# Eight experts in the last stage of a fused attention kernel: the second product turned round, the gate weights spread by DMA

## The chip, the cores and the metric

The kernel runs on one core of one Trainium2 chip. The engines of the core work side by side, each through its own queue of instructions in program order, and wait for one another by semaphores: TensorE (PE) multiplies, with its weight loads shown apart as PEld, VectorE (DVE) and ScalarE (ACT) do elementwise work, GpSimd (POOL) does elementwise work more slowly, SyncE (SP) issues the DMAs. The metric is the time on the device of one execution in microseconds (us), median of several runs; less is better.

## What is computed

The input is 32 sequences of 100 tokens with 128 features each. A first block (attention, cross attention, a small network), a second cross attention and a gated network run first; the stage that the change touches is the last one, a self-attention layer followed by a mixture of eight experts. Cut to what matters:

```python
def _moe(x, gW, gb, W1, b1, W2, b2):          # x: 3200 tokens x 128
    gates = softmax(xf @ gW + gb)              # 8 gates per token
    top2_scores, top2_idx = top_k(gates, 2)
    w = (one_hot(top2_idx, 8) * top2_scores[..., None]).sum(1)   # 3200 x 8, two of eight not zero
    h = relu(einsum('nd,edf->enf', xf, W1) + b1[:, None, :])     # f = 256
    y = einsum('enf,efd->end', h, W2) + b2[:, None, :]
    out = einsum('ne,end->nd', w, y)
```

The result is added to x, layer-normalised, scaled by a tanh of a gate and added to an earlier value. All eight experts are computed for every token, and the gate weight w sets what each adds.

## The kernel before

Three stages run one after another; `stage_c` is the last. It works on eight units of four sequences (400 tokens). Its first loop is self-attention, 64 pieces k of half a sequence's heads; its second loop is the experts, 64 pieces n, with u, e = divmod(n, 8): unit u, expert e. The order of instructions is written by hand, engine by engine, and nothing reorders it.

In the expert loop TensorE runs, for piece n, `expert(n)` and then `hidden(n + 2)`. `hidden` (line 1906) multiplies the tokens of unit u (YT, features on the partitions) with W1: two matmuls of 128x128 weights with 400 moving columns, into two of the PSUM banks 0 to 3. ScalarE's `rectify` (line 1682) adds the bias and clips to zero into HE, which has two places, so `rectify(n)` waits until `expert(n - 2)` is through. `expert` (line 1917) takes HE as weights, 100 tokens at a time, and W2 as the moving operand: eight matmuls of 128 moving columns, result with tokens on the partitions, in bank 4 or 5 by turns. VectorE's `add` (line 2096) multiplies that with the gate weight, which is one number per partition here, and adds it into U3, four instructions a piece. The records of the trace show each such float32 matmul twice (16 records for the eight matmuls, 4 for the two).

The bias b2 enters by way of the gate weights: `turn_weights` (line 1891) turns the 100x32 weights of a unit on TensorE, ScalarE copies them to WT (`weights_turned`, line 1673), `bias` (line 1754, reached through `project`) multiplies WT with B2 into bank 7, and VectorE's `first` (line 2089) starts U3 with that sum and the residual Y. Of the unit after, these stand behind pieces 3 and 5. After a unit's last piece VectorE takes the `moments` (lines 1993 to 1998), GpSimd the power for the standard deviation (`rstd`, line 1535), VectorE the `shift` (line 2003), ScalarE normalises (`leave`, line 1603, four instructions), GpSimd scales and adds (`leave`, lines 1566 and 1569), and SP stores (line 1522). A few steps of the attention of the last unit (`turn1`, `outer`, `turn2`, `gate`, the gate chain of units 6 and 7 on VectorE) stand between the first pieces.

Of the kernel before, what the change touches and what calls it, by code (L numbers as in the profile page):

```python
# [19 lines left out]
ALU = mybir.AluOpType  # L20
# [80 lines left out]
attx_psum b2_psum back_psum big_loaded c_chain c_cleared fe_ready fk_psum fk_ready fo_psum fpT_psum fpT_ready fq_psum  # L101
fq_ready fs_psum fu_ready fv_psum fv_ready gate_psum gate_used gexp_ready gsub_ready hb_ready kbd_ready moe_h_psum
moe_h_ready moe_y_psum moe_y_used os_ready out_ready out_scaled r_used sub_ready u_ready wT_psum wT_ready w_ready
wo_psum x_ready xb_ready xin_ready y_ready y_scaled
# [9 lines left out]
def build(nc, x, ctxn, ctxt, mask, wpack, cpack, rpack, kpack, w1, w2, b2, wgu, out):  # L114
    with ExitStack() as ctx:
# [16 lines left out]
        x1 = dram("x1_scratch", [T, BATCH, D])  # L132
        h3t = dram("h3t_scratch", [D, BATCH * T])
# [54 lines left out]
        stage_c(nc, t, x1, att, w1, w2, out)  # L188
# [1256 lines left out]
def stage_c(nc, t, x1, att, w1, w2, out):  # L1445

    with ExitStack() as ctx:
# [11 lines left out]
        loaded, stored = places("c_loaded", 2), places("c_stored", 2)  # L1459
# [20 lines left out]
        WT = sb("WT", [EXPERTS, 2, TG])  # L1480
        W1 = sb("W1", [D, FT * D])
# [24 lines left out]
        def _(sp):  # L1506
# [13 lines left out]
            for u in range(UNITS):  # L1520
# [77 lines left out]
        def _(act):  # L1598
# [70 lines left out]
            def weights_turned(u):  # L1669
                act.wait_ge(sem["wT_psum"], u + 1)  # L1670
                if u >= 2:
                    act.wait_ge(sem["b2_psum"], u - 1)
                nc.scalar.copy(WT[:, u % 2, :], bank(7, EXPERTS, TG)).then_inc(sem["wT_ready"], 1)

# [48 lines left out]
            weights_turned(0)  # L1723
            for n in range(PIECES):
# [19 lines left out]
        def _(pe):  # L1744
# [105 lines left out]
            def turn1(u):  # L1850
# [3 lines left out]
                elif u < LAST:  # L1854
                    pe.wait_ge(sem["gate_used"], u)
                else:
                    pe.wait_ge(sem["u_ready"], 1)
# [7 lines left out]
            def turn2(u):  # L1865
# [5 lines left out]
                else:  # L1871
                    pe.wait_ge(sem["u_ready"], 2)
# [7 lines left out]
            def turn_weights(u):  # L1880
                pe.wait_ge(sem["w_ready"], u + 1)
                if u == 0:
                    pe.wait_ge(sem["gate_used"], LAST)
                elif u == 1:
                    pe.wait_ge(sem["r_used"], UNITS)
                elif u == 2:
                    pe.wait_ge(sem["gate_used"], UNITS)
                else:
                    pe.wait_ge(sem["u_ready"], u)
                for j in range(GROUP):  # L1890
                    x_ = nc.tensor.transpose(bank(7, EXPERTS, T, j * T), gt[:, u, 6, j * EXPERTS:(j + 1) * EXPERTS], ident[0:T, 0:T])
                x_.then_inc(sem["wT_psum"], 1)

            def bias(u):
                pe.wait_ge(sem["wT_ready"], u + 1)
                project(7, WT[:, u % 2], t.B2[:, :], sem["b2_psum"])

# [346 lines left out]
```

## Time and profile before

| | us |
|---|---|
| median of 3 runs | 2406.93 |
| lowest and highest of them | 2406.34, 2409.48 |
| time of the profiled execution | 2401.97 |
| span of its trace | 2400.2 |
| TensorE busy in the span | 2028.5 (85%) |
| VectorE busy | 1583.8 (66%) |
| ScalarE busy | 1320.0 (55%) |
| expert loop, from its first hidden matmul (2157.5) to the end | 242.7 |

Times in the trace count from the start of the span. The profiled execution ran 5.0 us under the median of the three unprofiled ones, so a sum made in the trace is carried over to the median by adding that. The granted clock (PEclk) is TensorE's clock as a share of 2.4 GHz; 0.50 is its lower level, 1.2 GHz.

### The profile page before, as it was taken

How to read it: one execution, taken by the hardware profiler on the slowest of the kernel's cores; microseconds unless marked ns; L12 is line 12 of the kernel's file. 1: busy time of each engine (PE TensorE's matmuls, PEld its weight loads, DVE VectorE, ACT ScalarE, POOL GpSimd, SP SyncE). 2: the span in 40 equal slices, each digit the busy share in tenths (PEclk: the TensorE clock that was granted, in tenths of full speed). 3: DMA queues.
4: the chain of work that ended last, by engine and by line, in shares of the span. 5: the costliest groups of instructions: out<-in, count | busy, mean ns of one | idle time of the engine just before them, and what ended most of it. 6: DMA issues, size and time to landing. Idle time of an engine off the chain costs nothing. (4 is left out here: it accounts for less than half of the span.)

```text
span 2400.2 us, 45166 instructions
## 1 busy us (share of the span) xinstructions
PE 2028.5 (85%) x17914; PEld 1347.5 (56%) x17914; DVE 1583.8 (66%) x3854; ACT 1320.0 (55%) x2169; POOL 535.9 (22%) x476
## 2 busy tenths in 40 slices
PE   3779997466599999999999999999996888878997
PEld 2546665343355556556565555556564565656776
DVE  5844543787578878877877878878862566654443
ACT  3645554576246666666666666666673555543333
POOL 1410000553302212212222212212212233221111
PEclk9789997666589999999999999999997898879999
DMA  5026662000222313313323323313312110000000
GB/s 160 1 86 187 186 186 75 4 18 17 90 69 104 115 64 113 114 64 117 107 77 108 107 72 113 115 62 115 115 43 94 35 36 18 1 1 4 8 8 11
DMA packets 89104, 181.18 MB, mean 75 GB/s; under 512 B 5907, under 2 KB 63163, under 8 KB 88511
## 3 DMA queue, kind: packets, MB, share of 16 engines
q1 hardware_dynamic: 88894, 178.30, 22.6%
q8 instruction: 143, 2.34, 0.4%
q14 instruction: 67, 0.54, 0.1%
HBM read 95.24 MB, written 11.65 MB: 45 GB/s over the span
## 5 line engine op out<-in xcount | busy, mean ns | idle before, releaser
L1408 DVE TENSOR_REDUCE b_part_max<-psum 128x1 f32<-128x482 f32 (+3 forms) x1248 | 737.3, 650 | 187.6 <-PE psum L1285 173.6
L1198 ACT ACTIVATE b_PT<-psum 128x800 f32<-128x800 f32 x768 | 616.4, 836 | 386.0 <-PE psum L1304 380.0
L1285 PE MATMUL psum<-b_KH,b_QBD 64*128 64x482 f32 (+1 forms) x1152 | 421.4, 443 | 46.3 <-DVE b_part_max L1408 43.4
L1304 PE MATMUL psum<-b_QS,b_KS 64*128 64x200 f32 x3072 | 438.7, 288 | 0.5 <-ACT b_PT L1198 0.3
L1304 PEld LDWEIGHTS psum<-b_QS,b_KS 64*128 64x128 f32 x3072 | 339.6, 186 | 16.2 <-issue 12.1
L1320 PE MATMUL psum<-b_PT,b_V 128*32 128x200 f32 x6144 | 341.1, 339 | 0.6 <-ACT b_PT L1198 0.6
L1285 PEld LDWEIGHTS psum<-b_KH,b_QBD 64*128 64x128 f32 x1152 | 196.6, 188 | 198.0 <-DVE b_part_max L1408 118.6
L1121 POOL TENSOR_TENSOR b_KL<-b_KF,b_KH 128x1444 fp32r<-128x1444 f32 x32 | 106.8, 3337 | 691.9 <-PE psum L1304 669.7
L1320 PEld LDWEIGHTS psum<-b_PT,b_V 128*32 128x32 f32 x6144 | 159.9, 109 | 149.0 <-ACT b_PT L1198 82.3
L2096 DVE SCALAR_TENSOR_TENSOR c_U<-psum,c_gt,c_U 100x128 f32<-100x128 f32 x256 | 72.1, 344 | 129.0 <-PE psum L1917 128.8
L384 POOL TENSOR_TENSOR a_rs<-a_ve,a_half 100x4 f32<-100x4 f32 x48 | 50.0, 1041 | 420.7 <-DVE a_ve L757 420.6
L1917 PE MATMUL psum<-c_W,c_HE 128*100 128x128 f32 x1024 | 123.6, 274 | 14.1 <-ACT c_HE L1682 14.0
L1917 PEld LDWEIGHTS psum<-c_W,c_HE 128*100 128x100 f32 x1024 | 117.2, 167 | 31.8 <-ACT c_HE L1682 18.7
L1272 PE MATMUL psum<-W,b_CT 128*128 128x128 f32 (+1 forms) x768 | 117.7, 293 | 12.7 <-DVE b_part_max L1408 6.7
L804 DVE TENSOR_REDUCE a_peak<-psum 100x1 f32<-100x1446 f32 x32 | 53.2, 1664 | 105.3 <-PE psum L629 105.3
L1272 PEld LDWEIGHTS psum<-W,b_CT 128*128 128x128 f32 (+1 forms) x768 | 92.7, 188 | 41.4 <-DVE b_part_max L1408 37.4
L1682 ACT ACTIVATE c_HE<-psum,C 128x400 f32<-128x400 f32 x128 | 71.9, 587 | 78.9 <-PE psum L1906 75.9
L1646 ACT COPY c_PT<-psum 100x800 f32<-100x800 f32 x64 | 52.5, 821 | 102.0 <-PE psum L1810 102.0
L636 PE MATMUL psum<-a_P,a_CN 128*128 128x100 f32 (+1 forms) x768 | 108.0, 288 | 0.0
L1261 PE MATMUL psum<-b_CT,W 128*128 128x482 f32 (+1 forms) x192 | 101.2, 611 | 5.5 <-DVE b_QF L1382 1.5
L636 PEld LDWEIGHTS psum<-a_P,a_CN 128*128 128x128 f32 (+1 forms) x768 | 95.2, 195 | 18.7 <-issue 11.8
L1535 POOL TENSOR_TENSOR c_rs<-c_ve,c_half 100x4 f32<-100x4 f32 x24 | 24.4, 1015 | 337.0 <-DVE c_ve L1998 337.0
(274 smaller groups left out, 3204.3 us busy)
## 6 DMA issues: line engine op xcount, KB each, us to landing
b_KS<-b_KH SPq DMA_DIRECT2D x64, 722.0 KB
a_CT<-in_ctxt SPq DMA_DIRECT2D x32, 722.0 KB, 4.2
b_CT<-in_ctxt SPq DMA_DIRECT2D x32, 722.0 KB, 4.3
b_KS<-b_KL SPq DMA_DIRECT2D x32, 722.0 KB
a_CN<-in_ctxn SPq DMA_DIRECT2D x32, 704.0 KB
att_scratch<-b_AO SPq DMA_DIRECT2D x32, 200.0 KB, 1.9
c_AIN<-att_scratch SPq DMA_DIRECT2D x8, 800.0 KB
b_MB<-in_mask SPq DMA_DIRECT2D x32, 180.5 KB, 4.4
```

The source lines that it names most:

```text
L636: x_ = mm(bank(7, D, T, TG), CN[0:rows, m % 3, k, :], PTA[0:rows, m % 2, k, :], start=(k == 0), stop=(k == KT - 1))
L1121: pl.tensor_tensor(KL[:, :], KF[:, 0:S], KH[:, j % 2, :].bitcast(F32), ALU.subtract).then_inc(sem["kl_ready"], 1)
L1198: nc.scalar.activation(PT[:, kt % 2, 2 * a:2 * a + 2, :], psum[:, 2 * a:2 * a + 2, 0:TG], ACT.Exp).then_inc(sem["pt_ready"], 1)
L1261: m = mm(bank(b, D, size), w("xkT"), CT[:, j % 2, c:c + size], start=True, stop=True)
L1272: m = mm(bank(b, rows, D, (k % 4) * D), CT[:, j % 2, k * D:k * D + rows], w("xvT"), start=True, stop=True)
L1285: m = mm(bank(b, D, size), QBD[rows, j % 2, tile * D:(tile + 1) * D], KH[rows, j % 2, at_:at_ + size], start=True, stop=True)
L1304: m = mm(bank(p, D, 2 * T, (s % 2) * 2 * T), KS[rows, j % 2, s, kt * D:(kt + 1) * D], QS[rows, j % 2, s * 2 * T:(s + 1) * 2 * T], start=Tr ...
L1320: m = mm(psum[32 * r:32 * r + 32, 6, b * 2 * T:(b + 1) * 2 * T], V[:, j % 2, kt, 4 * b + r, :], PT[:, kt % 2, 2 * b + r // 2, (r % 2) * 2 ...
L1408: v.tensor_reduce(part_max[0:rows, q, c:c + 1], bank(b, rows, CHUNKS[c][1]), AX.X, ALU.max)\
L1682: nc.scalar.activation(HE[:, n % 2, f, :], bank((2 * n + f) % 4, D, TG), ACT.Relu, bias=t.C[:, c:c + 1]).then_inc(sem["moe_h_ready"], 1)
L1917: x_ = mm(bank(4 + n % 2, T, D, j * D), HE[:, n % 2, f, t.ts_(j)], W2[:, c * D:(c + 1) * D], start=(f == 0), stop=(f == 1))
L2096: last = v.scalar_tensor_tensor(out=U3[:, u % 2, j, :], in0=tok_bank(4 + n % 2)[:, j, :], scalar=gt[:, u, 6, j * EXPERTS + e:j * EXPERTS + ...
```

## The change

- `expert` takes W2 as the weights and HE as the moving operand: two matmuls of 400 columns a piece, into one bank (4 or 5) for the whole unit, features on the partitions. All eight experts add up in PSUM. The bias is one more matmul of 400 columns at the unit's end, B2 as weights and WT moving.
- With tokens along the columns, a gate weight is no longer one number per partition. So it is multiplied in ahead of the product: `weigh_hidden` on VectorE, two instructions a piece, multiplies HE in place with G, in which the weights of a unit stand on all 128 partitions.
- G is made by DMA: SP writes the 100x32 weights of a unit to DRAM in turned order, waits for that, and reads them back, once spread to 128 partitions (3200 numbers each) and once as the 8x400 WT. G uses the memory of AIN for even units and of KBD for odd ones, both free by then. All this stands in SP's queue ahead of the stores.
- At a unit's end ScalarE copies the sum to YF (`experts_kept`), TensorE turns it back into bank 7 (`turn_experts`, four transposes, behind piece 4 of the next unit), and VectorE's `gather` adds the residual and takes the moments, behind piece 5. `leave` of a unit stands two units later on ScalarE.
- `turn_weights`, `weights_turned`, `bias`, `first` and `add` are gone. The gate chain of units 6 and 7 is cut into parts behind different pieces.

```diff
+            def spread_gates(u):
+                sp.wait_ge(sem["w_ready"], u + 1)
+                sp.dma_start(gates[u].rearrange("(c k) -> k c", k=T),
+                             gt[:, u, 6, :],
+                             allow_slow_non_contiguous=True).then_inc(sem["w_stored"], 16)
+                sp.wait_ge(sem["w_stored"], 16 * (u + 1))
+                if u == 0:
+                    sp.wait_ge(sem["attx_psum"], UNITS)
+                if u == 1:
+                    sp.wait_ge(sem["fs_psum"], PIECES)
+                if u >= 2:
+                    sp.wait_ge(sem["moe_g_ready"], 2 * EXPERTS * (u - 1))
+                    sp.wait_ge(sem["yT_psum"], u - 1)
+                sp.dma_start(G[u % 2].rearrange("p e k -> p (e k)"), gates[u].partition_broadcast(D)).then_inc(g_loaded[u % 2], 16)
+                sp.dma_start(WT[:, u % 2, :], gates[u].rearrange("(e k) -> e k", e=EXPERTS)).then_inc(g_loaded[u % 2], 16)
...
+            for u in range(UNITS):
+                spread_gates(u)
+                if u >= 3:
+                    store(u - 3)
+            for u in range(UNITS - 3, UNITS):
+                store(u)
...
+            def experts_kept(u):
+                act.wait_ge(sem["yT_psum"], u + 1)
+                if u:
+                    act.wait_ge(sem["y_back_psum"], u)
+                nc.scalar.copy(YF[:, :], bank(4 + u % 2, D, TG)).then_inc(sem["yT_ready"], 1)
...
+                if e == 0 and u >= 2:
+                    leave(u - 2)
                 if e == 2 and u:
-                    leave(u - 1)
-                if e == 3 and u < LAST:
-                    weights_turned(u + 1)
+                    experts_kept(u - 1)
+            experts_kept(LAST)
+            leave(LAST - 1)
             leave(LAST)
...
+            def turn_experts(u):
+                pe.wait_ge(sem["yT_ready"], u + 1)
...
+                for j in range(GROUP):
+                    x_ = nc.tensor.transpose(bank(7, T, D, j * D), YF[:, t.ts_(j)], ident)
+                x_.then_inc(sem["y_back_psum"], 1)
...
             def expert(n):
-                e = n % EXPERTS
-                pe.wait_ge(sem["moe_h_ready"], 2 * n + 2)
-                if n >= 2:
-                    pe.wait_ge(sem["moe_y_used"], n - 1)
-                for j in range(GROUP):
-                    for f in range(2):
-                        c = 2 * e + f
-                        x_ = mm(bank(4 + n % 2, T, D, j * D), HE[:, n % 2, f, t.ts_(j)], W2[:, c * D:(c + 1) * D],
-                                start=(f == 0), stop=(f == 1))
+                u, e = divmod(n, EXPERTS)
+                b = bank(4 + u % 2, D, TG)
+                if e == 0 and u >= 2:
+                    pe.wait_ge(sem["yT_ready"], u - 1)
+                for f in range(2):
+                    pe.wait_ge(sem["moe_g_ready"], 2 * n + f + 1)
+                    c = 2 * e + f
+                    x_ = mm(b, W2[:, c * D:(c + 1) * D], HE[:, n % 2, f, :], start=(e == 0 and f == 0), stop=False,
+                            skip_group_check=True)
                 x_.then_inc(sem["moe_y_psum"], 1)
+                if e == EXPERTS - 1:
+                    pe.wait_ge(g_loaded[u % 2], 32 * (u // 2 + 1))
+                    mm(b, t.B2[:, :], WT[:, u % 2, :], start=False, stop=True, skip_group_check=True).then_inc(sem["yT_psum"], 1)
...
+            def weigh_hidden(n):
+                u, e = divmod(n, EXPERTS)
+                if e == 0:
+                    dve.wait_ge(g_loaded[u % 2], 32 * (u // 2 + 1))
+                for f in range(2):
+                    dve.wait_ge(sem["moe_h_ready"], 2 * n + f + 1)
+                    v.tensor_tensor(HE[:, n % 2, f, :], HE[:, n % 2, f, :], G[u % 2][:, e, :], ALU.mult).then_inc(sem["moe_g_ready"], 1)
```

TensorE, from behind piece 3 of a middle unit, before:

```order
L1891 MATMUL psum<-K,c_gt 8x100 x4
L1917 MATMUL psum<-c_W,c_HE 100x128 x8
L1906 MATMUL psum<-c_YT,c_W 128x400 x2
L1917 MATMUL psum<-c_W,c_HE 100x128 x8
L1906 MATMUL psum<-c_YT,c_W 128x400 x2
L1754 MATMUL psum<-B,c_WT 100x128 x4
L1917 MATMUL psum<-c_W,c_HE 100x128 x8
```

and after, from behind piece 4 (L1936 is `expert`, L1925 `hidden`, L1941 the bias, L1914 `turn_experts`):

```order
L1914 MATMUL psum<-K,c_YF 100x128 x4
L1936 MATMUL psum<-c_HE,c_W 128x400 x2
L1925 MATMUL psum<-c_YT,c_W 128x400 x2
L1936 MATMUL psum<-c_HE,c_W 128x400 x2
L1925 MATMUL psum<-c_YT,c_W 128x400 x2
L1936 MATMUL psum<-c_HE,c_W 128x400 x2
L1941 MATMUL psum<-c_WT,B 128x400
L1925 MATMUL psum<-c_YT,c_W 128x400 x2
```

Eight matmuls of 128 columns became two of 400, four small bias matmuls became one, and the turning of the weights became the turning of a finished unit.

VectorE, at the turn from one unit to the next, before:

```order
L2096 SCALAR_TENSOR_TENSOR c_U<-psum,c_gt,c_U 100x128 x8
L1993 BN_STATS c_stats<-c_U 100x6 x4
L181 MEMSET carrier 1x1
L1996 BN_AGGR c_mv<-c_stats 100x2 x4
L1998 TENSOR_SCALAR c_ve<-c_mv 100x4
L2089 TENSOR_TENSOR c_U<-psum,c_Y 100x512
L2096 SCALAR_TENSOR_TENSOR c_U<-psum,c_gt,c_U 100x128 x8
```

and after, from pieces 0 to 5 of a unit (L2110 is `weigh_hidden`, two rows a piece; L2116 and what follows it `gather` of the unit before; L2022 its `shift`):

```order
L2110 TENSOR_TENSOR c_HE<-c_HE,c_AIN 128x400 x12
L2116 TENSOR_TENSOR c_U<-psum,c_Y 100x512
L2012 BN_STATS c_stats<-c_U 100x6 x4
L182 MEMSET carrier 1x1
L2015 BN_AGGR c_mv<-c_stats 100x2 x4
L2017 TENSOR_SCALAR c_ve<-c_mv 100x4
L2110 TENSOR_TENSOR c_HE<-c_HE,c_AIN 128x400 x4
L2022 SCALAR_TENSOR_TENSOR c_nb<-c_mv,c_rs 100x4
```

The product now waits for VectorE ahead of it, where VectorE had worked behind it, and the end of a unit stands five pieces later.

SP, after its last load of the attention loop, has this from the fourth unit on (L1525 writes the turned weights, L1536 and L1537 read them back, L1541 stores a unit), where it had only the eight stores:

```order
L1525 DMA gates_scratch<-c_gt 100x32x1
L1536 DMA c_KBD<-gates_scratch 128x3200
L1537 DMA c_WT<-gates_scratch 8x400
L1541 DMA out_tokens<-c_OUT 100x512
L1525 DMA gates_scratch<-c_gt 100x32x1
L1536 DMA c_AIN<-gates_scratch 128x3200
L1537 DMA c_WT<-gates_scratch 8x400
```

Each unit has three DMAs more, and the store of unit u - 3 stands behind the reading back of unit u.

## Rows read from the trace of the kernel before

**Rows 1.** Busy time, granted clock and DMA by stretch: start:end, length, engines, PEclk.

```profile
core 0: us, PE busy (x) PEld busy (x) DVE busy (x) ACT busy (x) POOL busy (x), PEclk, DMA share, GB/s
2156.00:2160.00 4.00, 3.80 (x12) 2.64 (x13) 0.62 (x4) 0.00 (x0) 0.00 (x0) 0.50 0.00 0
2250.00:2300.00 50.00, 46.93 (x304) 36.82 (x303) 20.96 (x84) 20.34 (x40) 7.11 (x6) 1.00 0.03 9
```

**Rows 2.** Timeline, two pieces: start, length, engine, line, out<-in, [idle before <-releaser].

```profile
2250.79 1.91 PE L1917 MATMUL psum<-c_W,c_HE 128*100 128x128 f32 x16
...
2252.53 1.51 PE L1906 MATMUL psum<-c_YT,c_W 128*128 128x400 f32 x4
...
2253.41 1.26 ACT L1682 ACTIVATE c_HE<-psum,C 128x400 f32<-128x400 f32 x2 [1.83 <-PE psum L1906]
...
2253.88 1.91 PE L1917 MATMUL psum<-c_W,c_HE 128*100 128x128 f32 x16
```

**Rows 3.** Timeline of TensorE, one middle unit from its piece 4.

```profile
2238.17 0.51 PE L1891 MATMUL psum<-K,c_gt 100*8 100x100 f32 x4
2240.21 1.99 PE L1917 MATMUL psum<-c_W,c_HE 128*100 128x128 f32 x16 [1.53 <-ACT c_HE L1682]
...
2246.57 1.11 PE L1754 MATMUL psum<-B,c_WT 8*100 8x128 f32 x8
...
2268.29 1.99 PE L1917 MATMUL psum<-c_W,c_HE 128*100 128x128 f32 x16 [1.53 <-ACT c_HE L1682]
```

**Rows 4.** Timeline of TensorE, units 0 and 1.

```profile
2157.52 2.96 PE L1906 MATMUL psum<-c_YT,c_W 128*128 128x400 f32 x4
...
2163.17 1.99 PE L1917 MATMUL psum<-c_W,c_HE 128*100 128x128 f32 x16
...
2168.50 1.99 PE L1917 MATMUL psum<-c_W,c_HE 128*100 128x128 f32 x16 [1.65 <-ACT c_HE L1682]
...
2202.70 1.99 PE L1917 MATMUL psum<-c_W,c_HE 128*100 128x128 f32 x16 [1.56 <-ACT c_HE L1682]
...
2225.80 1.91 PE L1917 MATMUL psum<-c_W,c_HE 128*100 128x128 f32 x16
```

**Rows 5.** Timeline, from the last addition to the last store.

```profile
2388.88 1.12 DVE L2096 SCALAR_TENSOR_TENSOR c_U<-psum,c_gt,c_U 100x128 f32<-100x128 f32 x4 [0.62 <-PE psum L1917]
...
2391.61 1.02 POOL L1535 TENSOR_TENSOR c_rs<-c_ve,c_half 100x4 f32<-100x4 f32 x1 [14.18 <-DVE c_ve L1998]
...
2392.92 1.65 ACT L1603 ACTIVATE c_OUT<-c_U,c_nb,c_rs 100x128 f32<-100x128 f32 x4 [7.01 <-DVE c_nb L2003]
...
2397.27 0.29 SPq L1522 DMA_DIRECT2D out_tokens<-c_OUT  x1
```

**Rows 6.** VectorE groups by shape: line, op, shapes, count, busy us, mean ns, idle.

```profile
L2022 DVE TENSOR_TENSOR c_P<-psum,c_peak 100x400 f32<-100x400 f32 x128 | 67.4, 568 | 2.2
...
L2089 DVE TENSOR_TENSOR c_U<-psum,c_Y 100x512 f32<-100x512 f32 x8 | 5.5, 690 | 4.9 <-PE psum L1754 4.9
```

**Rows 7.** Timeline where VectorE and GpSimd read SBUF at once, and where not.

```profile
39.20 0.57 DVE L777 TENSOR_TENSOR a_P<-K,a_sm 100x400 f32<-100x400 f32 x1
...
1840.12 1.26 POOL L1539 TENSOR_TENSOR c_XIN<-c_XIN,c_rows 100x512 f32<-100x512 f32 x1
1840.19 1.22 DVE L2003 SCALAR_TENSOR_TENSOR c_nb<-c_mv,c_rs 100x4 f32<-100x4 f32 x1 [1.14 <-POOL c_rs L1535]
```

**Rows 8.** That VectorE line over the whole trace: duration ns min/median/max, first and last start.

```profile
L2003 DVE SCALAR_TENSOR_TENSOR c_nb<-c_mv,c_rs x24: 151/158/1220, 1840.2 to 2392.7; 100x4 f32<-100x4 f32 x24
```

**Rows 9.** DMA in 1787 to 1794, small copies alone: packets, MB, share of 16 engines.

```profile
q1 hardware_dynamic: 36, 0.01, 0.7%
```

**Rows 10.** DMA in 2397 to 2400.2, one store of 100 rows of 2 KB.

```profile
DMA packets 110, 0.20 MB, mean 64 GB/s; under 512 B 10, under 2 KB 10, under 8 KB 110
...
q1 hardware_dynamic: 110, 0.20, 21.7%
```

**Rows 11.** DMA in 2010 to 2018, one load of AIN and XIN.

```profile
q1 hardware_dynamic: 254, 1.02, 38.9%
```

More of the change, by code:

```diff
@@ L132, in build @@
         x1 = dram("x1_scratch", [T, BATCH, D])
+        gates = dram("gates_scratch", [UNITS, EXPERTS * TG])
         h3t = dram("h3t_scratch", [D, BATCH * T])
@@ L187, in build @@
         stage_b(nc, t, ctxt, mask, pen_dram, h3t, att)
-        stage_c(nc, t, x1, att, w1, w2, out)
+        stage_c(nc, t, x1, att, gates, w1, w2, out)
 def setup(nc, t, mask, wpack, cpack, rpack, kpack, b2, wgu, pen_dram):
@@ L1442, in _, with stage_c @@
             drain(END, 0, GROUPS - 1, GROUP + 1, "result", 0)
-def stage_c(nc, t, x1, att, w1, w2, out):
+def stage_c(nc, t, x1, att, gates, w1, w2, out):
     with ExitStack() as ctx:
@@ L1519, in _, with store @@
                 load(u)
-            for u in range(UNITS):
+            def spread_gates(u):
[13 more added lines that the diff above has]
+                sp.dma_start(WT[:, u % 2, :], gates[u].rearrange("(e k) -> e k", e=EXPERTS)).then_inc(g_loaded[u % 2], 16)
+            def store(u):
                 sp.wait_ge(sem["out_ready"], u + 1)
                 sp.dma_start(out[:, u * GROUP:(u + 1) * GROUP, :], OUT[:, u % 2, :, :]).then_inc(stored[u % 2], 16)
+            for u in range(UNITS):
[4 more added lines that the diff above has]
+                store(u)
             for place in range(2):
@@ L1959, in _ @@
             hidden(0)
-            turn_weights(0)
             hidden(1)
-            bias(0)
             for n in range(PIECES):
@@ L1975, in _ @@
                     gate(LAST)
-                if e == 3 and u < LAST:
-                    turn_weights(u + 1)
-                if e == 5 and u < LAST:
-                    bias(u + 1)
+                if e == 4 and u:
+                    turn_experts(u - 1)
+            turn_experts(LAST)
         @block.vector
@@ L2082, in gate_weights, with gather @@
                 link(last)
-                v.tensor_tensor(gt[:, u, 6, :], gt[:, u, 2, :], gt[:, u, 5, :], ALU.add).then_inc(sem["w_ready"], 1)
-            def first(u):
-                dve.wait_ge(sem["b2_psum"], u + 1)
+                v.tensor_tensor(gt[:, u, 6, :].rearrange("p (e j) -> p j e", j=GROUP), ge(u, 2), ge(u, 5), ALU.add).then_inc(sem["w_ready"], 1)
+            def weigh_hidden(n):
[5 more added lines that the diff above has]
+                    v.tensor_tensor(HE[:, n % 2, f, :], HE[:, n % 2, f, :], G[u % 2][:, e, :], ALU.mult).then_inc(sem["moe_g_ready"], 1)
+            def gather(u):
+                dve.wait_ge(sem["y_back_psum"], u + 1)
                 if u >= 2:
@@ L2090, in first @@
                 dve.wait_ge(sem["u_ready"], u + 1)
-            def add(n):
-                u, e = divmod(n, EXPERTS)
-                dve.wait_ge(sem["moe_y_psum"], n + 1)
-                for j in range(GROUP):
-                    last = v.scalar_tensor_tensor(out=U3[:, u % 2, j, :], in0=tok_bank(4 + n % 2)[:, j, :],
-                                                  scalar=gt[:, u, 6, j * EXPERTS + e:j * EXPERTS + e + 1], in1=U3[:, u % 2, j, :],
-                                                  op0=ALU.mult, op1=ALU.add)
-                last.then_inc(sem["moe_y_used"], 1)
-                dve.wait_ge(sem["moe_y_used"], n + 1)
+                moments(2, u, U3[:, u % 2])
             enter(0)
@@ L2132, in _ @@
                 u, e = divmod(n, EXPERTS)
-                if e == 0:
-                    first(u)
-                add(n)
+                weigh_hidden(n)
                 if n == 2:
@@ L2147, in _ @@
                     gate_top(LAST)
+                if n == EXPERTS + 6:
                     gate_place(LAST)
+                if n == EXPERTS + 7:
                     gate_weights(LAST)
-                if e == 1 and u:
+                if e == 5 and u:
+                    gather(u - 1)
+                if e == EXPERTS - 1 and u:
                     shift(2, u - 1)
-                if e == EXPERTS - 1:
-                    moments(2, u, U3[:, u % 2])
+            gather(LAST)
             shift(2, LAST)
```

42 lines of the change are left out of this document (14 added, 28 removed).

## The prediction

> **What bounds the kernel now.** I read the busy times by stretch first, then the timeline of two neighbouring pieces, then one whole unit, then the start and the end of the expert loop. In the middle of that loop TensorE is busy 46.93 of 50 us at the full clock, VectorE 20.96 and ScalarE 20.34 [rows 1]. The reader is to see in the timeline that nothing waits between two pieces: an expert product starts at 2250.79, the hidden product behind it at 2252.53, the next expert product at 2253.88 [rows 2]. So a piece costs TensorE 1.74 for the expert product and 1.35 for the hidden one, 3.09 us. A middle unit runs from 2240.21 to 2268.29, 28.08 us [rows 3]; eight pieces are 24.74, and the other 3.3 are the turning of the weights with the wait it causes (2238.17 to 2240.21, 2.04) and the bias that begins at 2246.57, with its bubbles the remaining 1.30. The loop is TensorE's, with one self-made wait a unit.
>
> **The product itself.** The new expert product has the shape of the hidden one: two matmuls of 128x128 weights by 400 columns. That shape is in the trace and costs 1.35 [rows 2]. It replaces 1.74, so a piece becomes 2.70, and 0.39 x 64 = 25 us go. This is less than the count of matmuls suggests (8 to 2), because both forms stream nearly the same columns: 8 x 128 against 2 x 400.
>
> **What goes and comes once a unit.** Out go the turning with its wait (2.04) and the bias (1.30). In come one matmul of 400 columns for the bias, half of 1.35, so 0.67, and four transposes. The nearest row is the four of 100 columns at 0.51 [rows 3]; these have 128, and I take 0.6 with the load in front. They don't wait: ScalarE copied YF two pieces earlier. What would be late next is the chain to the product, and I follow it from h, the start of hidden(n). ScalarE starts 0.88 behind h and needs 1.26 for both halves (2252.53 to 2253.41) [rows 2], so ends at h + 2.14. VectorE's multiplication of 128x400 with both operands in SBUF stands in the trace as 100x400 at 0.57 [rows 7]; with one from PSUM it is 0.568, and with 512 columns 0.690 [rows 6]. I take 0.57, bounds 0.43 (400 columns at what the last 112 of 512 cost, 0.122, with no start) and 0.69. The halves are ready at about h + 2.2 and h + 2.9. TensorE needs them at h + 4.05 and h + 4.72, since an expert product and a hidden one stand between. The slack is 1.8 us in either half. In an ordinary piece the two new instructions cost nothing, and VectorE's four of `add` are gone.
>
> Two things eat this slack. `gather` stands behind piece 5's multiplication and waits for the transposes, which start behind hidden(6). Counting from the start of piece 4's product, the transposes end at 3.3, VectorE sees it at 3.5, and gather takes 0.69 [rows 6] and 1.57 of moments (the last unit shows them from the last addition's end, 2390.0, to 2391.61 [rows 5]): 5.7. Only then does the multiplication of piece 6 start, ready at 6.3 where TensorE would begin at 6.0: a wait of 0.3 a unit (0.1 to 0.6 with the bounds above). The other is `leave` on ScalarE (1.65 [rows 5]), which delays the next clipping by 0.2: hidden by the slack. GpSimd's two additions after it I treat with the rivals. **A middle unit becomes 8 x 2.70 + 0.67 + 0.6 + 0.3 = 23.2 us**, 4.9 less than 28.08.
>
> **Units 0 and 1**, by the same recurrence. The loop still begins at 2157.52 with hidden(0), at the lower clock (0.50 [rows 1]), which ends near 2160. The first expert product waited for the weights' turning and the bias and stood at 2163.17 [rows 4]; now it stands behind hidden(1), at 2161.6. The wait of 1.65 at 2168.50 [rows 4] is ScalarE standing for `turn1` of the last unit ahead of its clipping; it stays and grows to about 2.1, VectorE's 0.57 being new in that chain. The one at 2202.70 (1.56 [rows 4]) has the same shape with `turn2`, and becomes 2.0. `residual` and the gate chain, cut in parts of about 1 us, fit into the slack in my working, save 0.3 behind `residual`. Piece by piece this puts the product of piece 8 at 2187.9 and of piece 16 at 2214.3, where it stood at 2225.80 [rows 4]: 11.5 us gained.
>
> **Units 2 to 7 and the end.** 2214.3 + 6 x 23.2 = 2353.5, less the two hidden products that the last two pieces don't have (2.7): the bias ends at 2350.8. From there: copy to YF 0.7 with its wait, transposes 1.0 from a standing start, gather 0.2 + 2.2, to 4.1. GpSimd meanwhile works on `leave` of unit 6, which ScalarE does only behind YF (0.7 + 1.65, then 2 x 1.27 on GpSimd, to 5.1), so the power of the last unit starts at 5.1. From the power's start to the store's issue it took 2391.61 to 2397.27, 5.66, and 2.93 from there to the span's end [rows 5]: 13.7 in all. Before, 11.3 lay behind the last addition's start at 2388.88. The tail is longer by the turning back and by GpSimd's unit 6. End: 2364.5 against 2400.2, **35.7 us less**. Against the profiled execution's 2401.97 that is 2366.3; the median of the runs stands 5.0 above that execution, so 2371.
>
> **The DMAs, taken at nothing.** The cover is time: SP sends a unit's weights while earlier units are computed. Writing them turned is 100 x 32 pieces of 4 bytes. A store of 100 rows shows 10 packets under 512 B, one for each of the engines that it ran on [rows 10]: ten engines, so 320 writes on each. Their price isn't in the trace. Small copies of up to 512 B: 0.7% of 16 x 7 us for 36 packets is 0.022 us each [rows 9]; 2 KB rows to DRAM: 21.7% of 16 x 3.2 us for 110 is 0.101 [rows 10]. With 2 us to land, the write takes S = 9 to 34 us. Reading back spread is 128 x 12.8 KB, 1.64 MB; at 38.9% of 16 x 8 us for 1.02 MB [rows 11], 49 us of engine time a MB, it holds the 16 engines for 5 us and lands 2 later. For units 0 to 2 everything is written long before. From unit 3 on SP's loop is: read back unit u (not before unit u - 2 is done), store unit u - 3, write unit u + 1, which queues behind the 5 us. One round costs S + 7 (5, 1 for the store, 1 of issues). It starts at the end of unit 0; the read-back of unit 7 lands at 5 S + 41 behind that, against 142 us for units 1 to 6 (26.4 for unit 1 and five of 23.2). So up to S = 20 nothing is lost, then 5 us for each us more; S = 27.5 eats the whole gain. I take a price near the small copies, since a 4-byte write moves less than any of them, doubled for its target in DRAM: 0.045, S = 16. No loss.
>
> **A rule of the skill against this.** The DMA row shows ten engines and no price for 4 bytes [rows 9, 10]. The Trainium skill, "DMA: Bandwidth & Descriptors", section "Rules for kernel authors", says that a strided last dimension becomes one descriptor per element, and section "Bandwidth" gives about 10.5 ns per packet as a floor for small ones; 3200 of them would be an estimated 34 us for S, and the kernel slower by about 33. No row here has such a write, so none agrees or contradicts; it is a load's figure that holds latency, which is why I give it little. It is the first rival below, and without it that rival's chance would be 0.10.
>
> **Rivals.** *The gate path becomes the bound* (the other side): at the upper row, 0.101 us a write, S = 34 and the loss is 5 x 34 - 101 = 69, so 2371 + 69 = 2440, 33 slower than now. For it: nothing of 4 bytes is in the trace, and writes of neighbouring tokens lie within the same few bytes of DRAM. Against: the cheap small packets. It decides from 27.5 us. Chance 0.14. *The same, but partly*: S between 20 and 27.5, 2371 to 2406. 0.07. *VectorE is held up by GpSimd.* A VectorE instruction with two SBUF inputs that takes 0.158 in the median [rows 8] took 1.22, to the end of a GpSimd addition of 1.26 beside it [rows 7]. The new multiplication has two SBUF inputs, and GpSimd's `leave` is two such additions a unit. I worked one meeting out: the second half is ready 0.8 before TensorE needs it. Were both additions to fall on both halves in the piece of gather too, about 1.4 a unit would be lost, 10 us: 2381. 0.13. The old addition read one operand from PSUM and never showed it. *The long columns bring nothing*, since the product doesn't stream as the hidden one does: then only the per-unit 1.8 and the start remain, 25 less, 2396. 0.02, since the shape is the same to the number.
>
> **Chances and range.** Forecast 0.61 (own range 2367 to 2378, from the bounds of the multiplication and the transposes), the others as above, 0.03 for what I don't see. Differences under 0.2% (4.8 us) are about what a measurement can't tell from no change. Faster 0.82, same 0.04 (the partial case near its end), slower 0.14. 2364 to 2400 holds all but the slow case, the end of the partial one and a little below.
>
> **What will show it.** In the trace after: expert and hidden products 2.70 apart in a middle unit; a unit of 23.2; four transposes behind piece 4 without a wait; a wait of about 0.3 at piece 6; VectorE's multiplications at 0.57, and up to 1.7 beside GpSimd; no wait of VectorE for a DMA at a unit's first piece. If units 3 to 7 begin with TensorE idle while VectorE waits for the read-back, the write's price is wrong, and SP's issues will stand S + 7 apart. A unit of 24.5 or more without a DMA wait would be the meeting with GpSimd.

## The result, and the profile after

| | before | after |
|---|---|---|
| median of the runs on one chip, us | 2408.2 (2406.34 to 2415.48) | 2372.97 (2364.85 to 2373.98) |
| time of the profiled execution | 2401.97 | 2372.8 |
| span of its trace | 2400.2 | 2371.0 |
| from the first hidden product of the expert loop to the end | 242.7 | 208.7 |
| one middle unit | 28.08 | 23.36 |

The ratio is 0.9851, with a 95% interval of 0.9828 to 0.9873: the changed kernel is 35.2 us faster by the medians, where 35.7 was forecast and 2371 written down. Compared loop against loop the two traces give 34.0. Their spans differ by only 29.2, because the loop began at 2162.31 in the one and at 2157.52 in the other; that difference is looked at under the second experiment.

First the busy times of a 50 us stretch in the middle of the loop (columns: stretch, length, busy time and count of PE, PEld, DVE, ACT, POOL, granted clock, DMA share, GB/s):

```profile
2250.00:2300.00 50.00, 49.81 (x151) 27.22 (x150) 25.56 (x59) 24.01 (x44) 10.53 (x6) 1.00 0.48 76
```

Against [rows 1] TensorE rose from 46.93 to 49.81: next to nothing waits in here any more. VectorE and ScalarE stand at half. The timeline of TensorE over one middle unit (start, duration, engine, line, operation; in brackets the idle time ahead and its releaser):

```profile
2233.75 0.60 PE L1914 MATMUL psum<-K,c_YF 128*100 128x128 f32 x4
2234.19 1.51 PE L1936 MATMUL psum<-c_HE,c_W 128*128 128x400 f32 x4
2235.53 1.51 PE L1925 MATMUL psum<-c_YT,c_W 128*128 128x400 f32 x4
2237.14 1.61 PE L1936 MATMUL psum<-c_HE,c_W 128*128 128x400 f32 x4
2238.58 1.51 PE L1925 MATMUL psum<-c_YT,c_W 128*128 128x400 f32 x4
...
2241.36 0.93 PE L1941 MATMUL psum<-c_WT,B 8*128 8x400 f32 x2
2242.23 1.61 PE L1925 MATMUL psum<-c_YT,c_W 128*128 128x400 f32 x4
...
2246.36 1.51 PE L1936 MATMUL psum<-c_HE,c_W 128*128 128x400 f32 x4
2247.71 1.51 PE L1925 MATMUL psum<-c_YT,c_W 128*128 128x400 f32 x4
2249.05 1.51 PE L1936 MATMUL psum<-c_HE,c_W 128*128 128x400 f32 x4
...
2257.55 1.51 PE L1936 MATMUL psum<-c_HE,c_W 128*128 128x400 f32 x4
```

These answer [rows 2, 3]. The expert product (L1936) and the hidden one (L1925) now take the same step, 1.34 each: 2246.36, 2247.71, 2249.05, so a piece is 2.69. The unit, from 2234.19 to 2257.55, is 23.36. The transposes (L1914) stand behind piece 4 and don't wait; they cost 0.44 (2233.75 to 2234.19). Behind them is the small wait of piece 6: the product that should follow 1.34 behind 2235.53 starts at 2237.14 instead of 2236.87, and its second half is late too (1.44 to the next instead of 1.34), 0.37 in all. The bias (L1941) starts about 0.1 late and takes 0.87 to the next product, and the step behind that is 0.1 longer too.

The start of the loop, the product of piece 10, and where unit 2 begins:

```profile
2162.31 5.59 PE L1925 MATMUL psum<-c_YT,c_W 128*128 128x400 f32 x8
2167.74 1.51 PE L1936 MATMUL psum<-c_HE,c_W 128*128 128x400 f32 x4
...
2172.71 1.61 PE L1936 MATMUL psum<-c_HE,c_W 128*128 128x400 f32 x4 [1.78 <-DVE c_HE L2110]
...
2201.49 1.61 PE L1936 MATMUL psum<-c_HE,c_W 128*128 128x400 f32 x4 [1.69 <-DVE c_HE L2110]
...
2220.32 1.51 PE L1936 MATMUL psum<-c_HE,c_W 128*128 128x400 f32 x4
```

The two waits of [rows 4] are still there, as 1.78 and 1.69, and their releaser is now VectorE's multiplication. The end of the loop, all engines, answers [rows 5]:

```profile
2356.81 0.93 PE L1941 MATMUL psum<-c_WT,B 8*128 8x400 f32 x2
...
2361.06 0.17 DVE L2017 TENSOR_SCALAR c_ve<-c_mv 100x4 f32<-100x4 f32 x1
...
2361.24 1.26 POOL L1595 TENSOR_TENSOR c_OUT<-c_OUT,c_X 100x512 f32<-100x512 f32 x1
2362.45 1.02 POOL L1561 TENSOR_TENSOR c_rs<-c_ve,c_half 100x4 f32<-100x4 f32 x1
```

The bias ends at 2357.74, 195.4 behind the start of the loop, and 13.3 remain. GpSimd is busy with unit 6 until 2362.50, where VectorE had the last variance ready at 2361.23, so the last power starts 1.2 late.

VectorE's multiplication (line and operation, count, shortest, median and longest ns, here for the even units; then what the multiplications of all units waited for, us and times):

```profile
L2110 DVE TENSOR_TENSOR c_HE<-c_HE,c_AIN x64: 559/574/1636, 2164.7 to 2331.4; 128x400 f32<-128x400 f32 x64
...
  ACT c_HE L1708: 66.7, 44
```

It takes 0.574 in the median, in the odd units too, and the trace lists no wait for a DMA: G was always there in time. The queue of SP shows why (issues of read-back, write, and next read-back):

```profile
2289.10 0.34 SPq L1536 DMA_DIRECT2D c_AIN<-gates_scratch  x1
...
2292.03 0.34 SPq L1525 DMA_DIRECT2D gates_scratch<-c_gt  x1
2312.46 0.34 SPq L1536 DMA_DIRECT2D c_KBD<-gates_scratch  x1
```

The packets of a stretch that holds one read-back and one write, 2193 to 2215, and of the part of it in which the write runs, 2198 to 2203, show the price of the 4-byte writes:

```profile
q1 hardware_dynamic: 3370, 1.66, 41.8%
```

```profile
DMA packets 3245, 0.12 MB, mean 23 GB/s; under 512 B 3230, under 2 KB 3238, under 8 KB 3238
...
q1 hardware_dynamic: 3245, 0.12, 93.4%
```

41.8% of 16 x 22 us is 147 us of packet time; the read-back at the 49 us a MB of [rows 11] is 81 of it, and 66 remain for 3200 writes, 0.021 us each: the lower of my two bounds. Divided by ten engines that would be 6.6 us. The write was shorter still: all but a few of its packets lie between 2198.3 and 2202.5, about 4 us. The ten engines of [rows 10] could be busy for 62.5% of 16 at most, and the share was 93.4%, from 2201 to 2202 even 129%, so the recorded times of these packets overlap on an engine. With some 2.5 us to land (with three writes the next read-back was issued that long behind their last packet), S was about 7 for one write, and not 16. The Trainium skill, "DMA: Bandwidth & Descriptors", section "Rules for kernel authors", says that a strided last dimension becomes one descriptor per element; the trace agrees, with 3230 small packets. Its figure of 10.5 ns a packet (section "Bandwidth") would have made an estimated 34 us of them one behind the other; here a lone write took an eighth of that.

### The profile page after: what moved, and what is told of

Same layout as the page of the kernel before. It is cut to its first block and busy times, and to the rows that moved or that the text cites. A ratio compares the mean times of both kernels' runs of the same rounds, so it can differ in the third digit from the quotient of the medians.

```text
span 2371.0 us, 43329 instructions
## 1 busy us (share of the span) xinstructions
PE 2013.5 (85%) x17098; PEld 1287.2 (54%) x17098; DVE 1590.6 (67%) x3726; ACT 1323.8 (56%) x2169; POOL 549.7 (23%) x476
## 5 line engine op out<-in xcount | busy, mean ns | idle before, releaser
L1286 PE MATMUL psum<-b_KH,b_QBD 64*128 64x482 f32 (+1 forms) x1152 | 421.5, 443 | 46.3 <-DVE b_part_max L1409 43.4
L1561 POOL TENSOR_TENSOR c_rs<-c_ve,c_half 100x4 f32<-100x4 f32 x24 | 36.1, 1504 | 306.7 <-DVE c_ve L2017 306.7
L1936 PE MATMUL psum<-c_HE,c_W 128*128 128x400 f32 x256 | 97.4, 504 | 4.2 <-DVE c_HE L2110 3.5
L1925 PE MATMUL psum<-c_YT,c_W 128*128 128x400 f32 x256 | 99.7, 514 | 0.0
L623 PE MATMUL psum<-a_CT,a_RT 128*100 128x482 f32 x192 | 89.6, 604 | 0.6 <-ACT a_RT L445 0.6
```

The source lines that it names most:

```text
L623: mm(bank(3 * (m % 2) + c, T, CHUNK), RT[:, u, t.ts_(j)], CT[:, m % 3, c * CHUNK:(c + 1) * CHUNK], start=True, stop=True).then_inc(sem["s2 ...
L1286: m = mm(bank(b, D, size), QBD[rows, j % 2, tile * D:(tile + 1) * D], KH[rows, j % 2, at_:at_ + size], start=True, stop=True)
L1925: mm(bank((2 * n + f) % 4, D, TG), W1[:, c * D:(c + 1) * D], YT[:, u, :], start=True, stop=True).then_inc(sem["moe_h_psum"], 1)
L1936: x_ = mm(b, W2[:, c * D:(c + 1) * D], HE[:, n % 2, f, :], start=(e == 0 and f == 0), stop=False, skip_group_check=True)
```

## The experiments

**One line of the kernel before.** How much of the gain needed the change at all? In the kernel before, ScalarE copied the turned weights of the next unit ahead of a clipping that TensorE needed sooner.

```diff
-                if e == 3 and u < LAST:
+                if e == 4 and u < LAST:
                     weights_turned(u + 1)
```

> The kernel before with one edit: ScalarE copies the turned weights behind the clipping of piece 4 instead of piece 3, so that it doesn't stand and wait with that clipping behind it. Nothing else. It asks how much of the gain is that self-made wait and how much the product. Theory (by the sum: 1.53 us of wait a unit, seven units, and the product 0.39 a piece): 10 to 11 us faster than the kernel before, a middle unit 26.5 instead of 28.08, so the change keeps 25 us of its own. Rival (the wait moves to another place, to the bias that waits for the copy): under 4 us, a new wait ahead of the bias matmuls in the trace.

Measured: 2390.59 (2389.45 to 2398.3), ratio to the kernel before 0.9945 (0.9924 to 0.9967), which is 15.8 us less by the medians; and in the trace a loop of 230.3, 12.4 less. Both are more than the 10 to 11 expected. TensorE's transposes of the weights, one unit apart, and the product behind the first of them, which no longer waits:

```profile
2234.51 0.51 PE L1891 MATMUL psum<-K,c_gt 100*8 100x100 f32 x4
2234.86 1.91 PE L1917 MATMUL psum<-c_W,c_HE 128*100 128x128 f32 x16
...
2260.82 0.51 PE L1891 MATMUL psum<-K,c_gt 100*8 100x100 f32 x4
```

A unit is 26.31, 1.77 less than 28.08. So about 12 of the 34 us of the loop came from a wait that one moved copy takes away as well, and the change is worth the other 22. That speaks against the story that the change won by its longer matmuls alone. The 22 are less than the 25 of the product, because the change pays with steps of its own: the transposes, the wait at piece 6 and a tail that is 2 us longer than the old one.

**The kernel after once more.** Did the change move the start of the loop by 4.8 us?

> The changed kernel once more, unchanged, as the measure for the others of this set. Theory (the loop gains, and what the two profiled executions differ by ahead of the loop is chance): its expert loop, from the first hidden matmul to the end of the span, is again 208 to 210 us (208.7 in its first trace, 242.7 before the change), while the start of the loop in the trace may lie some us off 2162.3. Rival (the change costs 4.8 us ahead of the loop, by its writes and reads of the weights beside the attention): the loop starts again 4 to 5 us later than in a trace of the kernel before, at 2162 or more.

Measured: 2369.37 (2366.83 to 2376.44), ratio 0.9851 (0.9828 to 0.9875). Its loop began at 2159.04 and lasted 209.6. Over all ten traces that hold the new expert loop it began between 2157.17 and 2169.93, so a start late by 4.8 is within what one kernel does. A third repetition:

> The kernel after, unchanged, on the same chip as the version with the three moves: about 2370, ratio to the kernel before 0.985; loop from the first hidden product to the span's end 209.

Measured: 2371.67 (2368.05 to 2374.21), ratio 0.9847 (0.9826 to 0.9868), start at 2163.56, loop 208.8. The two traces with the old loop began it at 2157.52 and 2157.40, among the earliest, so the starts alone don't settle whether the change costs something ahead of the loop. The medians speak against it: in three sets of runs they fell by 35.2, 37.0 and 34.6 us, where the loops alone give 34.0, 33.1 and 33.9; a cost of 4.8 would have left 29. With intervals of some 5 us to either side a smaller cost isn't excluded. Loops, not spans, are compared from here on.

**More of the element-wise write.** The main rival was the price of the 4-byte writes. Each unit's write is issued two, three or five times, the copies to spare places:

```diff
                 sp.wait_ge(sem["w_ready"], u + 1)
-                sp.dma_start(gates[u].rearrange("(c k) -> k c", k=T),
-                             gt[:, u, 6, :],
-                             allow_slow_non_contiguous=True).then_inc(sem["w_stored"], 16)
-                sp.wait_ge(sem["w_stored"], 16 * (u + 1))
+                for extra in range(3):
+                    sp.dma_start(gates[u + extra * UNITS].rearrange("(c k) -> k c", k=T),
+                                 gt[:, u, 6, :],
+                                 allow_slow_non_contiguous=True).then_inc(sem["w_stored"], 16)
+                sp.wait_ge(sem["w_stored"], 3 * 16 * (u + 1))
```

> The changed kernel with each unit's turned write issued three times, to three places in DRAM, and waited for as a whole; the reading back is as it was. Theory (a 4-byte write takes an engine 0.021 us, as the packets of the changed kernel's trace say, so one write takes S = 6.6 us and 2 to land, three take 20 + 2): at the edge of what the loop hides, S = 22, so by 5 S - 101 a loss of 9 us at most, 0 to 9. Rival (a write costs what the prediction took, 0.045, S = 16, three of them 45): 5 x 45 - 101, 125 us slower than the changed kernel.

> The kernel after with each unit's turned write issued twice (the second copy to a spare place in DRAM), nothing else. With it issued three times SP's rounds stood 30.9 us apart and 20 us were lost, where S + 7 with S = 3 x 6.6 + 2 gives 28.8. Theory A (a round is 9 + 7.3 for each write): 23.6 us for two writes, just above the unit's 23.36: 0 to 2 us lost, about 2371 to 2373, read-backs 23.4 to 23.8 apart. Rival B (a round is 10.3 for each write, since the read-back runs beside them): 20.6, nothing lost, and read-backs at TensorE's pace as in the kernel after.

> The kernel after with each unit's turned write issued five times. Theory A (a round is 9 + 7.3 for each write): read-backs 45.5 apart, and five to six rounds of 14.6 more than with three writes: about 2388 + 80 = 2470. Rival B (10.3 for each write): 51.5 apart, about 2388 + 113 = 2500.

Measured: 2380.61 with two, 2388.49 with three, 2468.8 with five writes (one run each; on the chip of the first and the last the kernel before took 2410.97). The loops are 208.8, 229.0 and 306.6, that is 0, 20 and 98 us lost. The high total of the first is a late start of its loop, at 2169.93. SP's read-backs, two neighbours each with two, three and five writes, and for three what VectorE's multiplications waited for (us, times):

```profile
2298.73 0.34 SPq L1537 DMA_DIRECT2D c_AIN<-gates_scratch  x1
...
2323.73 0.34 SPq L1537 DMA_DIRECT2D c_KBD<-gates_scratch  x1
```

```profile
2279.63 0.34 SPq L1537 DMA_DIRECT2D c_KBD<-gates_scratch  x1
...
2280.74 16.87 SPq L1526 DMA_DIRECT2D gates_scratch<-c_gt  x3
2310.87 0.34 SPq L1537 DMA_DIRECT2D c_AIN<-gates_scratch  x1
```

```profile
  DMA c_WT<-gates_scratch: 25.1, 3
```

```profile
2375.66 0.34 SPq L1537 DMA_DIRECT2D c_AIN<-gates_scratch  x1
...
2422.37 0.34 SPq L1537 DMA_DIRECT2D c_KBD<-gates_scratch  x1
```

With two writes the rounds of the later units are 23.4, 23.5, 25.1 and 25.0: first TensorE's pace, then longer than a unit, and the lead of the first units still covers that. With three they are 30.0 to 31.7, on average 31.1 in the last four, and with five 46.3 (mean of five). That is 6 to 8 us for each further write. With three VectorE waits for the weights, and with five 104.7 us in five waits. A round with one write can't be read from the pace, which is TensorE's; from its packets (read-back issued at 2242.39, last packet of the write near 2253.3, some 2.5 to land) I estimate 14, far under the 23.36 of a unit.

So the rival's mechanism is real and its place is the one named; only S is about 7 for one write, where the loss begins at 20. The prediction's rule, a round of S + 7 and a loss of 5 S - 101, can be tested with S read from the rounds: 31.1 - 7 = 24.1 for three writes gives 19.5 where 20 were measured, 46.3 - 7 = 39.3 for five gives 95.5 where it was 98, and 18 for two gives no loss. The form was right. My expectations held less well. The 0 to 9 us for three writes missed, having used 6.6 us a write and one landing alone, which made S = 22. For two writes theory A (rounds of 23.6) is nearer than B (20.6), and the last two rounds exceed both. For five, 2470 met 2468.8 and 2500 fell.

**GpSimd's two additions cut to 4 columns** (the output isn't scaled or added in full):

```diff
-pl.tensor_tensor(OUT[:, u % 2, :, :], OUT[:, u % 2, :, :], wide(1), ALU.mult).then_inc(sem["out_scaled"], 1)
+pl.tensor_tensor(OUT[:, u % 2, 0, 0:4], OUT[:, u % 2, 0, 0:4], rows[:, 1, 0:4], ALU.mult).then_inc(sem["out_scaled"], 1)
...
-pl.tensor_tensor(OUT[:, u % 2, :, :], OUT[:, u % 2, :, :], X[:, u, :, :], ALU.add).then_inc(sem["out_ready"], 1)
+pl.tensor_tensor(OUT[:, u % 2, 0, 0:4], OUT[:, u % 2, 0, 0:4], X[:, u, 0, 0:4], ALU.add).then_inc(sem["out_ready"], 1)
```

> The changed kernel with GpSimd's two additions at the end of each unit cut from 512 columns to 4, so the output is not scaled and added in full. It asks whether the meetings of VectorE and GpSimd at SBUF cost the loop anything. Theory (they are hidden by the slack of 1.8 us): VectorE's multiplications lose their long ones, all near 0.57 us save beside the power, the middle unit stays 23.36 us, and only the end is shorter, by the additions of the last two units, some 3 us. Rival: the unit gets shorter by 0.5 us or more.

Measured: 2376.89 (one run, loop start at 2169.54), loop 205.6, 3 to 4 less than after. The transposes of two neighbouring units:

```profile
2241.08 0.60 PE L1914 MATMUL psum<-K,c_YF 128*100 128x128 f32 x4
...
2264.44 0.60 PE L1914 MATMUL psum<-K,c_YF 128*100 128x128 f32 x4
```

The unit stays 23.36, and the last transposes begin 196.1 behind the loop's start as in the kernel after (196.0): the gain is all in the tail, where the additions stand on the path. The meetings do happen, as the kernel after shows on VectorE and GpSimd:

```profile
2243.68 1.27 POOL L1595 TENSOR_TENSOR c_OUT<-c_OUT,c_X 100x512 f32<-100x512 f32 x1
2243.83 2.04 DVE L2110 TENSOR_TENSOR c_HE<-c_HE,c_KBD 128x400 f32<-128x400 f32 x2 [2.50 <-ACT c_HE L1708]
```

Two multiplications take 2.04 instead of 1.15: the first starts 0.15 behind GpSimd's addition and takes 1.55, ending 0.43 behind the addition's end. They end at 2245.87, and the product that reads them starts at 2246.36: the slack swallows it, as worked out. The rival's loss of 10 us is refuted.

**VectorE's multiplication cut to 4 columns** (the hidden layer is left unweighted but for these) and, the other way, **done twice**, first into a spare tile (the added wait is for VectorE's own earlier write of that tile):

```diff
-v.tensor_tensor(HE[:, n % 2, f, :], HE[:, n % 2, f, :], G[u % 2][:, e, :], ALU.mult).then_inc(sem["moe_g_ready"], 1)
+v.tensor_tensor(HE[:, n % 2, f, 0:4], HE[:, n % 2, f, 0:4], G[u % 2][:, e, 0:4], ALU.mult).then_inc(sem["moe_g_ready"], 1)
```

```diff
+if n:
+    dve.wait_ge(sem["spare"], 2 * n + f - 1)
...
+v.tensor_tensor(SPARE[:, f, :], HE[:, n % 2, f, :], G[u % 2][:, e, :], ALU.mult).then_inc(sem["spare"], 1)
 v.tensor_tensor(HE[:, n % 2, f, :], HE[:, n % 2, f, :], G[u % 2][:, e, :], ALU.mult).then_inc(sem["moe_g_ready"], 1)
```

> The kernel after with VectorE's multiplication cut to 4 of 400 columns; the rest of the hidden layer is left unweighted, so the output isn't the reference's; all waits and DMAs stay. Theory (the multiplication lies beside TensorE's work): the middle unit is 23.1 instead of 23.36, its wait at piece 6 being gone; 0.5 each at the first product and at pieces 1 and 10; in all 3 to 4 us less than the kernel after, loop 205 to 206. Rival (the multiplication costs in every piece): a piece under 2.69 and a loop of 200 or less.

> The kernel after with each of VectorE's multiplications done twice, first into a spare tile (two more instructions a piece, 0.57 each). Theory (a slack of 1.8 us in either half, less what gather takes): from h, the start of the hidden product, the halves are ready at h + 2.65 and h + 3.8 and needed at h + 4.05 and h + 4.72, so an ordinary piece still is 2.69; only the piece behind gather loses some 0.6 for each half (about 1.2 a unit, 9 us), and unit 0 and 1 with the gate chain some 3 to 8 more: about 2385 (2378 to 2392), a middle unit 24.5. Rival (there is hardly any slack): every piece becomes longer by 0.3 or more, a unit 26 or more, and the time is above 2392.

Measured (one run each), cut: 2362.65, loop 203.7, 5.0 less than after, where 3 to 4 were expected; unit 22.99, since only the 0.37 at piece 6 is gone (seven times, 2.6; another 1.3 is the clock's earlier rise at the start, and 0.8 the shorter waits at pieces 1 and 10). Twice: 2383.12, loop 223.1, 14.4 more; unit 24.16. About 5 of the 14.4 are the 0.80 in each of the six units 2 to 7. From the first product to piece 16 it is 8.8 more, part of which is the clock: behind the longer waits of pieces 1 and 10 it fell, as the last section shows. TensorE around piece 6 with the multiplication done twice:

```profile
2240.41 1.51 PE L1926 MATMUL psum<-c_YT,c_W 128*128 128x400 f32 x4
2242.52 1.91 PE L1937 MATMUL psum<-c_HE,c_W 128*128 128x400 f32 x4 [0.60 <-DVE c_HE L2114]
2244.26 1.51 PE L1926 MATMUL psum<-c_YT,c_W 128*128 128x400 f32 x4
2245.61 1.51 PE L1937 MATMUL psum<-c_HE,c_W 128*128 128x400 f32 x4
```

Behind the hidden product of 2240.41 the next comes 2.11 later instead of 1.34, and the one behind that 1.74 later: 1.17 lost where 1.2 was worked out. All other pieces of this unit stay at 2.69 (2244.26 to 2245.61 is again 1.34), though VectorE's work in them doubled. In a middle unit the multiplication is beside TensorE's work in seven pieces of eight, and there is slack for a second one there, as the 1.8 us of the prediction have it.

**Three moves in the kernel after**, made from the waits that its trace still shows:

```diff
-                if n == 0:
+                if n == 1:
                     turned1(LAST)
...
-                if n == EXPERTS + 1:
+                if n == EXPERTS + 2:
                     turned2(LAST)
...
-            experts_kept(LAST)
             leave(LAST - 1)
+            experts_kept(LAST)
             leave(LAST)
...
                 v.tensor_tensor(U3[:, u % 2, :, :], tok_bank(7), Y[:, u, :, :], ALU.add).then_inc(sem["u_ready"], 1)
+
+            def measure(u):
                 dve.wait_ge(sem["u_ready"], u + 1)
                 moments(2, u, U3[:, u % 2])
...
                 if e == 5 and u:
                     gather(u - 1)
+                if e == 6 and u:
+                    measure(u - 1)
...
             gather(LAST)
+            measure(LAST)
```

> The kernel after with three moves: ScalarE copies turned1 of the last unit one piece later (behind the clipping of piece 1) and turned2 one piece later (behind that of piece 10); gather keeps only its addition at piece 5 and takes its moments behind the multiplication of piece 6; at the end ScalarE scales unit 6 before it copies the last YF. Theory (the three waits are the order's own, each removed by letting the chain h -> clipping -> multiplication go first): the waits at pieces 1 and 10 (1.78 and 1.69 us in the trace after) and the 0.26 at piece 6 of seven units go, 5.3 us, and GpSimd's unit 6 is done about 1 us earlier at the end: the loop from the first hidden product to the span's end 203 instead of 209, the time 6 us below the kernel after (ratio 0.9975). Rival (a later copy makes the next reader late: the waits only change place): under 2 us gained, and a wait of over 1 us of TensorE or VectorE at pieces 2 to 4 or 11 to 13.

Measured: 2362.77 (2358.31 to 2369.95), ratio to the kernel before 0.9822 (0.9797 to 0.9847), where the kernel after had 0.9847 on the same chip: 8.9 us less by the medians. The loop is 201.2, 7.6 less than in the repetition beside it; 203, and a time 6 us lower, were expected. TensorE's first two expert products of the loop, and two transposes one unit apart:

```profile
2163.40 1.51 PE L1936 MATMUL psum<-c_HE,c_W 128*128 128x400 f32 x4
...
2166.43 1.53 PE L1936 MATMUL psum<-c_HE,c_W 128*128 128x400 f32 x4
...
2225.09 0.60 PE L1914 MATMUL psum<-K,c_YF 128*100 128x128 f32 x4
...
2248.09 0.60 PE L1914 MATMUL psum<-K,c_YF 128*100 128x128 f32 x4
```

The second expert product comes 3.03 behind the first instead of 4.97, the unit is 23.00, and within the loop TensorE has one wait left that the timeline marks, for the last YF. The stretch from the first expert product to the end of the last bias is 6.5 shorter, of which the waits are 1.78 + 1.69 + 7 x 0.37 = 6.1; the tail is 0.7 shorter, and 0.4 is an earlier rise of the clock. The three waits were the order's own, not the change's price. This is the fastest version measured; the interval of its ratio overlaps that of the kernel after, so the 7.6 us rest on the traces.

## Why the prediction was right, and where it was off

- **The product.** 1.74 was to become 1.35, a piece 2.70: the trace has 1.34 and 2.69. Both forms stream nearly the same columns, and the shape in the trace of before gave the price of the new one.
- **The unit.** 23.2 was the forecast, 23.36 came. The transposes were over-priced (0.6 for 0.44). The bias was under-priced: 0.67 for 0.87, with another 0.1 ahead of it and 0.1 behind it. The wait behind gather was 0.37 for 0.3.
- **The first product.** Forecast 4.1 behind the start of the loop, measured 5.4: the term that was off most. I had let the clock rise where it rose in [rows 1, 4]. In the kernel after it stayed at 1.2 GHz longer (windows from the start of the loop, clock behind PE, PEld, DVE, ACT, POOL):

```profile
2163.00:2166.00 3.00, 3.00 (x6) 1.56 (x5) 0.72 (x3) 1.19 (x2) 0.00 (x0) 0.50 0.00 0
2166.00:2169.00 3.00, 3.00 (x7) 1.56 (x7) 0.57 (x1) 0.00 (x0) 0.00 (x0) 0.72 0.00 0
```

  The rise moves from run to run: this distance is 4.15 in the kernel with the cut multiplication, 4.58, 5.43 and 5.48 in three executions of the kernel after. Whether the old loop would have had the late rise as often isn't settled; both of its traces rose early, and two are too few.
- **Units 0 and 1.** From the first product to piece 16, 52.7 was worked out and 52.6 measured. The waits at pieces 1 and 10 were forecast as 2.1 and 2.0 and are 1.78 and 1.69.
- **The tail.** 13.7 forecast, 13.3 measured, with GpSimd's unit 6 ahead of the last power, as said.
- **The DMAs, taken at nothing.** They cost nothing. The price I took was over twice the true one (S = 16 for about 7), on the safe side; the rule for a loss was confirmed by three and five writes within 3 us. No row of before showed that the true price lay at the cheap end of two bounds that are a factor of four apart. The prediction gave 0.21 to a price that costs something, so that it came out cheap is in part luck.
- **Rivals.** The gate path as the bound needs three writes in place of one; the meeting with GpSimd exists and is hidden; the long columns brought what they should.
- **The sum.** 35.7 forecast on the loop, 34.0 measured: 1.3 of the 1.7 is the clock at the start, 1.0 the units, and the tail gave 0.4 back. That the medians differ by 35.2, nearer to 35.7 than the loop does, is chance: the four runs of either kernel spread over 9 us, and the before median moved by 1.3 with its fourth run.

## What to carry to other kernels

Before pricing a new form, look for the same shape elsewhere in the trace: here that gave the product's step to 0.01 us, and with it 25 of the 36. A helper path of DMAs needs a round time and a slack, both from rows, and a price with both ends, with the loss at the upper end written down beside its threshold. That keeps the risk in sight; it doesn't remove it. And look at the order first: a copy issued one piece too early cost 12 us in the old kernel, and two more of them were still in the new one (3.5 us).

## What was not expected of the hardware

- **A slow write held SP in the issue itself.** Alone, the 4-byte write was issued in 0.34 us; three in a row kept SP for 16.87 (the row above), five for 31 to 33. One issue of the kernel with three writes (shortest, median and longest ns of all 24) took up to 9.5 us:

```profile
L1526 SPq DMA_DIRECT2D gates_scratch<-c_gt x24: 289/7098/9518, 2012.5 to 2321.0; - x24
```

  What stands behind several such writes in SP's queue is issued only after that.
- **GpSimd's small power instruction was held up by VectorE.** It took 1.017 us in every unit of the kernel before. In the kernel after its row over the expert loop (shortest, median, longest ns), and with the multiplication cut to 4 columns:

```profile
L1561 POOL TENSOR_TENSOR c_rs<-c_ve,c_half x9: 1017/2727/2730, 2178.9 to 2362.5; 100x4 f32<-100x4 f32 x9
```

```profile
L1561 POOL TENSOR_TENSOR c_rs<-c_ve,c_half x9: 1017/1017/1017, 2172.0 to 2352.3; 100x4 f32<-100x4 f32 x9
```

  With GpSimd's own additions cut instead, the median stayed 2.717. So it is VectorE's run beside it, of four multiplications with two SBUF inputs, that adds 1.7 us. In one unit of the kernel after the power ran from 2236.68 to 2239.41, and VectorE's row is:

```profile
2236.51 2.02 DVE L2110 TENSOR_TENSOR c_HE<-c_HE,c_AIN 128x400 f32<-128x400 f32 x4
```

  The power ended 0.9 behind the last of the four. The Trainium skill, "SBUF — State Buffer", section "SBUF: two separate sides", calls the shared port pair an exclusive lock that blocks the loser for a whole instruction; the traces agree in both directions (a multiplication of 0.57 grew to 1.55 beside GpSimd's addition; 1.7 more for the power here). They show one thing beyond it: the power stayed held over four instructions, not one. It cost nothing, as nobody needed the power's result within that time.
- **The clock fell again in one execution** of the kernel after, in the window behind the wait at piece 1 (0.76, then 0.68 of full speed), and the rows of the two products there add up to 4.85 us instead of 3.12. In the other two executions the two products behind the same wait of 1.78 took their usual time. With the multiplication done twice the waits at pieces 1 and 10 are 2.33 and 2.25 long, and the clock fell behind both (0.72 and 0.62, 0.75 and 0.60).
